# A two-layer graph network on one core: one more gathered tile of layer one taken over by TensorE in every second group

## What is computed

```
h = relu(layernorm(x))
for b in range(8):  xb = h @ V[b];  m += comp[etype][:, b] * xb[src]
m = m * edge_weight
agg = segment_sum(m, dst)
h1 = relu(agg + bias + h @ loop_w)
```

## Time and profile before

| | us |
|---|---|
| median of 3 runs | 2015.04 (2015.01 to 2017.97) |
| the profiled execution | 2014.24 |
| its span | 2012.5 |
| PE / DVE / POOL / ACT busy in the span | 1703.1 / 1447.5 / 1392.8 / 357.2 |
| edges of chunk 0 (start) to the last issue of a layer-one gather | 82.4 to 976.9 |

### The profile page before, as it was taken

How to read it: one execution, slowest core, us unless ns; L and a number is a source line. 1 busy time by engine, 2 the same in 40 slices (tenths; PEclk the granted TensorE clock), 3 DMA queues, 4 the chain that set the end, 5 groups by cost and what they waited for, 6 DMA issues and landing times. The chain is left out here.

```text
span 2012.5 us, 41270 instructions
## 1 busy us (share of the span) xinstructions
PE 1703.1 (85%) x12580; PEld 1219.9 (61%) x12581; DVE 1447.5 (72%) x2327; ACT 357.2 (18%) x869; POOL 1392.8 (69%) x1516
## 2 busy tenths in 40 slices
PE   1488878888888888888569989999999999978898
PEld 1366556556656556566447666766677766755664
DVE  7898888888888888887578867776677776722533
ACT  2032222222222222222101101011011110111300
POOL 5777777777777777777477777777777777777000
PEclk8589889889889889889689999999999999978999
DMA  5334334334344343342222222233333332334473
GB/s 150 93 98 114 95 99 108 94 101 104 93 104 103 93 106 102 95 109 73 74 57 64 63 60 62 61 85 97 88 91 88 83 100 78 93 94 129 149 238 120
DMA packets 195273, 196.69 MB, mean 98 GB/s; under 512 B 109132, under 2 KB 158681, under 8 KB 195178
## 3 DMA queue, kind: packets, MB, share of 16 engines
q0 software_dynamic: 45408, 93.09, 18.2%
q1 hardware_dynamic: 141718, 98.31, 16.8%
q10 hardware_dynamic: 8052, 4.04, 0.7%
HBM read 169.75 MB, written 25.57 MB: 97 GB/s over the span
## 5 line engine op out<-in xcount | busy, mean ns | idle before, releaser
L831 POOL DMA_INDIRECT ring<-h_rows,rel_idx x1302 | 1248.6, 959 | 388.7 <-issue 363.1
L1016 DVE TENSOR_TENSOR rel_pick<-rel_src_row,dve_bank 128x1664 bf16<-128x1664 int32 (+1 forms) x268 | 485.8, 1813 | 131.3 <-PE rel_ps_p L1267 62.1
L1342 PE MATMUL rel_ps_z<-rel_C,ring 128*128 128x56 f32 x3100 | 409.9, 280 | 132.5 <-DVE ring L1032 75.8
L1342 PEld LDWEIGHTS rel_ps_z<-rel_C,ring 128*128 128x128 f32 x3100 | 394.8, 198 | 179.2 <-issue 169.1
L1440 ACT ACTIVATE rel_ZT<-rel_ps_z 128x304 f32 x292 | 114.2, 426 | 1038.0 <-PE rel_ps_z L1342 1036.4
L1280 PE MATMUL rel_ps_p<-rel_h_parts,rel_pick 128*128 128x384 bf16 x1150 | 266.5, 363 | 0.0
L1267 PE MATMUL rel_ps_p<-rel_h_parts,rel_pick 128*128 128x384 bf16 x1375 | 235.8, 328 | 23.4 <-DVE rel_h_parts L1004 22.3
L1430 ACT ACTIVATE rel_A<-rel_ps_a 128x500 f32 x292 | 165.5, 603 | 391.5 <-PE rel_ps_a L1219 202.9
L1267 PEld LDWEIGHTS rel_ps_p<-rel_h_parts,rel_pick 128*128 128x128 bf16 x1375 | 133.4, 100 | 114.8 <-issue 27.9
L1267 PE MATMUL carried<-rel_h_parts,rel_pick 128*128 128x384 bf16 x1100 | 190.5, 331 | 2.4 <-DVE rel_pick L1016 2.4
L1219 PE MATMUL rel_ps_a<-rel_M,rel_lo 128*128 128x175 bf16 x784 | 157.3, 296 | 38.9 <-DVE rel_M L983 38.2
(11 more groups left out here) (233 smaller groups left out, 1722.7 us busy)
## 6 DMA issues: line engine op xcount, KB each, us to landing
ring<-h_rows,rel_idx POOLq DMA_INDIRECT x1302
A_slabs<-rel_A SPq DMA_DIRECT2D x25, 800.0 KB
A_slot<-A_slabs SPq DMA_DIRECT2D x25, 800.0 KB, 4.5
rel_types<-edge_types SPq DMA_DIRECT2D x97, 200.0 KB
early_slot<-A_slabs SPq DMA_DIRECT2D x18, 896.0 KB, 6.1
rel_src_row<-in_src_dram SPq DMA_DIRECT2D x134, 64.0 KB, 3.2
last_slot<-A_slabs SPq DMA_DIRECT2D x4, 512.0 KB, 5.7
ring<-h_rows,idx_table POOLq DMA_INDIRECT x117
```

The source lines that it names most:

```text
L831: g_.indirect_dma_start(ring[:, s * CHUNK + i, :], None, rows_in, bass.IndirectOffsetOnAxis(ap=idx[which][:, n:n + 1], axis=0)).then_inc(l ...
L1016: v.tensor_tensor(pick[:, b0:b0 + n, :], src_row[s][:, :].unsqueeze(1).to_broadcast(shape), node_ids[:, b0:b0 + n].unsqueeze(2).to_broadca ...
L1342: ins = m_.matmul(bank(ps_z[s], NB)[:, :, bass.ds(at[i], TW)], ring[:, first + i, :], C[s][:, i, :, :], start=False, stop=(i == n - 1))
```

## The change

In every odd group of layer one the last tile of the third chunk is picked too and no longer gathered. Ring slot 6 of 8 (`THIRD`) then holds seven gathered tiles. The third and fourth chunk of an odd group now do a whole pick each on TensorE (`pick_quarter`: 7, 6, 6, 6 matmuls; the third piece stands ahead of the edges, in the fourth chunk behind the degree sum). SyncE loads one more row of sources for each pair of groups into `extra_row`. On VectorE the third chunk's pick matrix is made in the second and third chunk; the fourth chunk's is made at the end of the third chunk (first half) and in the fourth chunk (second half), behind `keep_picked` of the third chunk's pick; and the first half for the next group's first pick moves from ahead of the scaling to behind the degree. Even groups keep their order. The groups concerned are 1, 3, ..., 23: twelve tiles. The core of the diff (the rest renames counts to suit):

```diff
+PICK_QUARTERS = ((0, 7), (7, 13), (13, 19), (19, 25))
...
+THIRD = SLOTS_RING - 2
...
-        def number(g, j):
-
-            return 2 * g - 2 + j // 2
+        def number(g, j, parity, pair):
+
+            return 2 * g - 2 + j // 2 + pair + (1 if parity == 1 and j == 3 else 0)
+
+        def nearby(g, j, parity, by):
+
+            parity, pair = (parity + by) % 2, loop[1] + (parity + by) // 2
+            return number(g + by, j, parity, pair)
+
+        def is_third(parity, j):
+
+            return layer == 0 and parity == 1 and j == 2
 
         def gathers(s, late=False):
 
             if layer == 1 and s == EXTRA and not late:
...
-            return CHUNK if late else CHUNK - (1 if layer == 1 else s % 2)
+            return CHUNK if late else CHUNK - (1 if layer == 1 or s == THIRD else s % 2)
...
-            return half * (gathers(s) * 16)
+            return half * (CHUNK * 16 - 4) + 4 * ((s // 2 + ahead) % (SLOTS_RING // 2))
...
+                def load_third(g, before):
+
+                    after(sp, pick_ready, before)
+                    rows = io["src"].rearrange("(a n) -> a n", a=1)
+                    sp.dma_start(extra_row[:, :], rows[:, bass.ds((g * CPG + 2) * (CHUNK * P) + (CHUNK - 1) * P, P)].to_broadcast([P, P]))\
+                      .then_inc(extra_in, 16)
 
...
+                                k = nearby(g, behind[1], parity, 0 if j == 2 else -1)
+                                load_sources(*behind, 0 if is_group(behind[0], 0) else 2 * k + 2)
+                            if parity == 0 and j == 0 and not is_group(g, GROUPS - 1):
+                                load_third(g + 1, 2 * nearby(g, 3, parity, -1) + 2)
...
+                        third = nearby(g, 2, parity, 0)
                         if j % 2 == 0:
-                            behind = (g, 1) if j == 2 else (g - 1, 3)
                             if not (isinstance(g, int) and not first_picks(c - 1)):
-                                keep_picked(number(*behind), 0, (parity * CPG + j - 1) % SLOTS_RING * CHUNK + CHUNK - 1)
-                            if not (isinstance(g, int) and not first_picks(c + 1)):
-                                make_pick(number(g, j + 1), j // 2, g - 1, (1,))
+                                behind = nearby(g, 1, parity, 0) if j == 2 else nearby(g, 3, parity, -1)
+                                keep_picked(behind, 0, (parity * CPG + j - 1) % SLOTS_RING * CHUNK + CHUNK - 1)
+                            if is_third(parity, j):
+                                make_extra(third, loop[1], 1)
+                            elif not (isinstance(g, int) and not first_picks(c + 1)):
+                                make_pick(nearby(g, j + 1, parity, 0), j // 2, g - 1, (1,))
+                        elif parity == 1 and j == 1:
+                            make_extra(third, loop[1], 0)
+                        elif parity == 1:
+                            keep_picked(third, 0, THIRD * CHUNK + CHUNK - 1)
+                            make_pick(nearby(g, 3, parity, 0), 1, g - 1, (1,))
+                        elif j == 1:
+                            if not (isinstance(g, int) and not first_picks(c + 2)):
+                                make_pick(nearby(g, 3, parity, 0), 1, g - 1, (0,))
                         else:
-                            ahead = (g, 3) if j == 1 else (g + 1, 1)
-                            if not (isinstance(g, int) and not first_picks(c + 2)):
-                                make_pick(number(*ahead), ahead[1] // 2, ahead[0] - 1, (0,))
+                            make_pick(nearby(g, 1, parity, 1), 0, g, (0,))
...
+                    if is_third(parity, j):
+                        make_pick(nearby(g, 3, parity, 0), 1, g - 1, (0,))
...
+                        if parity == 1 and not is_group(g, GROUPS - 2):
+                            make_pick(nearby(g, 1, parity, 1), 0, g, (0,))
...
+            def pick_quarter(c, which):
+
+                b0, b1 = PICK_QUARTERS[which]
+                if which == 0:
+                    after(pe, row_ready, c)
+                if which % 2 == 0:
+                    pe.wait_ge(pick_ready, 2 * c + (1 + which // 2))
+                for b in range(b0, b1):
+                    ins = m_.matmul(ps_p[0][:, 0:3 * P], pick[:, b, :], h_parts[:, b, :, :].rearrange("p c n -> p (c n)"),
+                                    start=(b == 0), stop=(b == SRC_BLOCKS - 1))
+                if which % 2:
+                    ins.then_inc(picked, 1)
+
...
+                    quarters = picks_here and parity == 1 and j >= 2
+                    nth = nearby(g, j if quarters else j // 2 * 2 + 1, parity, 0) if picks_here else None
+                    if quarters:
+                        pick_quarter(nth, 0)
+                    elif picks_here:
                         if is_group(g, 1) and j == 0:
                             pe.wait_ge(split_done, GROUPS // SPLIT_GROUPS)
                         pick_sixth(nth, j, 0)
                     if makes(g, j):
...
+                    if quarters:
+                        pick_quarter(nth, 1)
...
+                    if quarters:
+                        pick_quarter(nth, 2)
...
+                        if quarters and i == HALF:
+                            pick_quarter(nth, 3)
+                        elif picks_here and i == HALF:
                             pick_sixth(nth, j, 2)
-                        if layer == 0 and i == CHUNK - 1 and j % 2 == 1 and not (isinstance(c, int) and not first_picks(c)):
-                            pe.wait_ge(row_ready, number(g, j) + 1)
+                        if picks_here and i == CHUNK - 1 and (j % 2 == 1 or quarters):
+                            pe.wait_ge(row_ready, nth + 1)
```

19 lines of the change are left out of this document (8 added, 11 removed).

## The result

| | median us | runs |
|---|---|---|
| before | 2015.03 (2012.69 to 2017.97) | 4 |
| with the change | 2087.26 (2083.32 to 2094.24) | 4 |

The ratio is 1.0368, 95% interval 1.0348 to 1.0389: 3.7% slower, 72 us. 2074 was forecast, with 2055 to 2095 as the range. The profiled execution took 2085.96 us, its span is 2084.1 against 2012.5. I call those runs disturbed. They show pauses on TensorE that nothing in the trace releases and a lower granted clock, and neither their sizes nor their order is used for the argument.

What follows compares the result with a forecast made beforehand. The prediction took a ring of waits between PE and DVE, not POOL's gathers, as the bound. 5.8 us in each of 11 pairs, 63.8, less 5 at the layer's end gave +59 us on 2015.0: 2074 us, range 2055 to 2095.

Steps and rivals of the forecast that it cites:

- the ring between PE and DVE: Layer one: PE waits 68.4 us for DVE's picked row and 31.6 for `M`, DVE 49.5 for PE's degree sum.
- Rival 1: Gathers are the bound or the ring has room: layer one ends 15 us earlier, 2000 us; chance 0.04.
- The odd group, 5.8 us forecast: Group 13's times: the added-up row's release to PE moves from 594.85 to 600.65, 5.8 us in a pair.
- the slow stretch would start later: Fourth chunk on PE: slow clock from 1.1 to 4.8 us after resumption, seven picks slow at 0.32 us each.
- groups 1 to 21 have 11 such pairs, 63.8 us: Layer one: group 13's delay of 5.8 us a pair, used for all 11 pairs, adds up to 63.8 us.
- from 600.65 on PE and DVE do what they did: Rest of a pair, after the next group's first added-up row: unchanged, so the 5.8 us delay simply adds up.
- The last odd group, -5 forecast: Group 23 at layer one's end: gather waits of 3.29 and 3.04 us go; -5 us, bounds -1 to -7.
- most of the slow time after it: Behind the 3.04 us gather wait: 16 edge matmuls took 3.63 us, 1.5 more than in steady state.
- The clock: PE's clock after the new waits, not shown by the trace: likeliest as many slow spans as now.
- the upper bound's 7.4: A pair with one more slow span, 1.6 us: 7.4 x 11 - 1 = +80, 2095 us.
- Rival 2: PE's clock stays up with denser picks: delay only 1.3 us a pair, 2024 us; chance 0.04.
- Rival 3: Extra source row lands late on SP's queue, or clock low through the whole fourth chunk: 2109 us; chance 0.07.

Runs made afterwards that it cites:

- Experiment 5: The change with all its picking, but the third chunk's last tile gathered as before and the picked row unread: 2087.94 us, ratio 1.037 to the kernel before.
- experiment 11: The kernel before with the fourth chunk's degree sum moved right behind the slab's matmuls, on an undisturbed chip: 2015.63 us against 2013.85, ratio 1.0009.
- Experiment 12: The change with both first pick-matrix halves made behind the added-up rows on VectorE, undisturbed: 2028.26 us, ratio 1.0065 to the kernel before.
- all_moved_third: The change with both pick halves behind the added-up rows and the degree sum right behind the slab, undisturbed: 2006.9 us, ratio 0.9954 to before.
- experiment 10: The same run as all_moved_third: the change with both pick halves and the degree sum moved, undisturbed: 2006.9 us against 2016.02, ratio 0.9954.
- the first move: The change with only the half for the next group's first pick made behind that group's added-up row: 2611.5 us against 2592.34 for before, disturbed.
- before_degree_early: The kernel before with the fourth chunk's degree sum right behind the slab's matmuls; first run, disturbed: 2550.58 us against 2592.34, ratio 0.9828.
- all_moved: The change with both pick halves behind the added-up rows and the degree sum early; first run, disturbed: 2556.71 us against 2592.34, ratio 0.9858.

## Why the prediction was right, and where it was off

**The bound.** That the ring between PE and DVE sets the pace, and that the gathers don't, held. Experiment 5 shows it for the change from one side, experiment 11 from the other: once the ring is shortened, POOL's pace appears. Rival 1 would have needed room in the ring or gathers that bind: a pair 6.9 us longer excludes the one, experiment 5 the other.

**The odd group, 5.8 us forecast.** 6.0 were measured. DVE's stretch from 615.34 to the third chunk's row, and PE's resumption at 628.15, are 12.81 us apart; 573.89 to 586.60, 12.71, were forecast. The wait there was to be some 3 us, it is 3.32. The wait for the degree sum was to be about 4.3, it is 4.83. What was off cancels in part, so the nearness of 6.0 to 5.8 is partly luck: the slow stretch began at once and not 1.1 us after the resumption, so that the slab's matmuls start 1.45 us behind the edge tile (628.15 to 629.60), where I put 0.83; and the degree and one-hot ahead of the last addition cost less, since DVE has no 0.45 us pause on issue there any more. That the slow stretch would start later was an argument from one row; by it the way from the last edge tile to the slab's matmuls was put 0.6 us too short. Experiment 12 confirms that these places, and not the added work as such, make most of the loss: with the same number of picks and 1.8 us of DVE's work moved twice, a pair is 5.1 us shorter.

**The step that was mis-sized is the multiplication "groups 1 to 21 have 11 such pairs, 63.8 us".** The prediction took it that "from 600.65 on PE and DVE do what they did". They don't quite. In the mean of the last eight pairs up to group 21, from picked row to picked row: fourth chunk of the odd group to second chunk of the even one 18.28 us in place of 17.83, on to its fourth chunk 19.55 in place of 19.43, on to the odd group's second chunk 17.87 in place of 17.72, and on to its fourth 26.22 in place of 20.05. The sum is 6.9 a pair, so 75.4 over the eleven in place of 63.8: 11.6 us too little. Of the missing 1.1 us a pair, 0.2 is the step above. Another 0.1 to 0.2 is the choice of group 13, whose last stretch (20.19) is longer than the mean (20.05); nor do the 41 waits of the earlier trace rows have like lengths, as the prediction says: about half of them, the second chunks', are 0.2 us. 0.45 is the slow clock behind the fourth chunk's row: from 642.31 to the product at 647.34 are 5.03 us, from 594.85 to that at 599.41 only 4.56, and from there on both kernels take 13.2 us to the next row. What is left, some 0.3 in the even group, I haven't traced to single rows.

**The last odd group, -5 forecast.** Measured +0.6 and -4.4, together -3.8, which looks nearer than it is. At the end of chunk 96's edges the gain stands at 2.8 us (+0.6 and -3.4), and the rest of the -3.8 comes from later parts, which the prediction took as unchanged. The two gather waits of the earlier trace rows are gone as forecast. I had counted "most of the slow time after it" as gone too, 1.5 us for the 16 edge matmuls. They take 2.75 now in place of 3.63, so 0.9 of it.

**The clock.** It was the part that the trace didn't show, and I took as many slow spans as before. The 6.9 us of a pair are nearer to the upper bound's 7.4 (one more such span) than to 5.8. Rival 2 said that with denser picks the clock stays up. The mean went the other way, 0.91 to 0.88; but the matmuls didn't become denser either (2949 in place of 3039 in 440 us). That rival rested on a sentence of the Trainium skill, "TensorE: Matmul & The Clock Gate", section "What's actually happening", by which activity releases the throttle. More matmuls in a pair didn't do so here, since the pauses grew with them. The trace doesn't contradict the sentence: in `all_moved_third`, where PE's waits are short, 120 to 520 us have 3093 matmuls at 0.97, and the same stretch of the kernel before 2808 at 0.91. Which is cause and which effect these rows don't tell. What the page's section "HAM oscillation — how this bites in real kernels" puts first, pauses between bursts, fits in so far as every slow stretch shown here follows a pause. But the length of the pause doesn't settle it: in experiment 12 the picks are fast behind 1.04 us and slow behind 1.00.

**Rival 3** (the extra row late, or a slow clock through the whole fourth chunk) didn't occur. DVE's wait ahead of `rel_pick` at 621.49 is released by PE, as are all 11 (4.2 us in sum), and the clock is back up in the sequence behind 634.

**The signs named beforehand.** Twelve gathers fewer; POOL waiting longer than 0.3 us; a pair of about 81 us (81.9); some 3 us of wait at the third chunk; the waits for `M` halved (31.6 to 13.7); the degree wait at about 4.3 (4.8); no gather wait at the end. All came; that POOL's longer pauses are waits for PE's edges is inferred, since the rows name no releaser.

**The gathers' worth.** The forecast said that one gather less counts at the layer's end alone. In the change it doesn't count even there (experiment 5): the end's waits go because PE comes later. It isn't true of a kernel with a shorter ring: from experiment 11 to 10 the last gather comes 8.2 us earlier and the time is 9 us less (11 by the ratios, each against its own kernel before). Of the 15 us that twelve gathers take, some 7 don't arrive. POOL's pauses sum to 187.5 us there, where twelve fewer of 0.3 would leave 183.3, so 4.2 us of the missing are longer pauses, up to 2.1 us, in which POOL is held. The rest, some 3 us, stands in the gathers' own busy time: 642.6 us for 659 gathers there, 649.6 for 670 in experiment 11, where 11 fewer at the same mean would be 638.9. Why they are longer is open. Also left open is what the first move does alone, undisturbed, what the early degree sum alone gives to the change, and what the saved gathers give to the kernel before.

## What to carry to other kernels

Where two in-order engines wait for each other in turn, look at the place of an instruction before counting the work. Here two instructions of 1.8 us each, moved from right behind such a wait to a place ahead of the next one, were worth 5.1 us a pair, with no work removed. A saving on an engine that nobody waits for was worth nothing until the ring was shorter than that engine's pace, and some 9 us afterwards; so shorten the ring first and take the saving second. And price a new pause on TensorE as a range: what follows it may run at half the clock or not (seven picks 2.42 us or 1.31), and in these traces the length of the pause alone didn't tell which.

## What the runs showed of the hardware that was not expected

The granted clock was at 0.50 from the first matmul behind pauses of 3.32 and 3.63 us (the change); behind one of 3.57 us the first two edge matmuls still ran at full pace (before); behind one of 1.58 us the slow stretch came 1.1 us after the resumption. Behind pauses of 1.04 and 1.00 us in two pairs of the same kernel, seven picks took 1.31 and 2.42 us. A pause alone, told by its length, did not decide the clock.

On two chips the same program took 2592 and 2566 us in place of 2015, with pauses of up to 2.1 us inside sequences of matmuls that nothing released, and a mean clock of 0.81 against 0.91 in the kernel before. On them `before_degree_early` was 1.7 and 1.8% faster than before, and undisturbed it was the same; it was ahead of `all_moved` there by a little, and behind it undisturbed. In these kernels a ratio didn't carry over from such a chip, even with both kernels run side by side on it.
